# Later requests for feed-forward weight units and a new order of transpositions and copies in a fused GNN, attention and feed-forward kernel

## The reference

```python
def _fff(x, node_w, node_b, w1, b1, w2, b2):
    ...
    for _ in range(DEPTH):                      # 4 levels: a leaf of 16 for every row
        pw = node_w[cur]
        score = jnp.einsum('nd,nd->n', xf, pw) + node_b[cur]
        cur = 2 * cur + 1 + (score >= 0).astype(jnp.int32)
    leaf = cur - N_NODES
    sel = jax.nn.one_hot(leaf, N_LEAVES, dtype=xf.dtype)
    hidden_all = jax.nn.relu(jnp.einsum('nd,ldh->lnh', xf, w1) + b1[:, None, :])
    hidden = hidden_all * sel.T[:, :, None]
    out = jnp.einsum('lnh,lho->no', hidden, w2) + sel @ b2
...
attn = jax.nn.softmax(jnp.einsum('bqd,bkd->bqk', q, k) * scale, axis=-1)
return jnp.einsum('bqk,bkd->bqd', attn, v)
```

## Time and profile before

| | |
|---|---|
| median of 3 runs | 715.13 us (715.1 to 717.05) |
| the profiled execution | 714.04 us |
| its span, first to last instruction | 712.3 us |
| PE (matmul) busy | 694.5 us, 97% |
| DVE (VectorE) busy | 478.6 us, 67% |
| ACT (ScalarE) busy | 403.2 us, 57% |
| POOL (GpSimd) busy | 253.2 us, 36% |
| granted TensorE clock | 1.0 in every stretch |

### The profile page before, as it was taken

The page is one execution under the profiler, slowest core; times in us unless marked ns, Lnnn a source line. Parts: engine busy times, 40 slices in busy tenths (PEclk is TensorE's granted clock), DMA queues, the critical chain, the costliest instruction groups (busy, mean ns, idle before and its releaser), DMA issues.

```text
span 712.3 us, 11790 instructions
## 1 busy us (share of the span) xinstructions
PE 694.5 (97%) x4447; PEld 654.9 (92%) x4447; DVE 478.6 (67%) x965; ACT 403.2 (57%) x702; POOL 253.2 (36%) x232
## 2 busy tenths in 40 slices
PE   8999999999999999999999999999999899989998
PEld 8899999998999999999999999998899897869896
DVE  6778766784777477766666566658675567786744
ACT  5555646555565465758686775522432666675541
POOL 5744312222232322227122263654006841341240
PEclk9999999999999999999999999999999999999999
DMA  6832563422323223231312242333167879997242
GB/s 234 330 115 91 206 237 121 177 90 93 122 104 119 88 92 119 93 119 60 119 59 86 85 183 93 131 122 118 60 237 264 277 297 380 357 363 282 104 155 98
DMA packets 25096, 115.39 MB, mean 162 GB/s; under 512 B 7248, under 2 KB 7680, under 8 KB 15968
## 3 DMA queue, kind: packets, MB, share of 16 engines
q1 hardware_dynamic: 14144, 85.05, 32.5%
q0 software_dynamic: 10464, 29.39, 11.6%
q10 hardware_dynamic: 432, 0.20, 0.1%
HBM read 99.35 MB, written 22.49 MB: 171 GB/s over the span
## 4 chain that ended last, share of the span: by engine, by line
PE 82%; DVE 9%; ACT 4%; DMA 3%; issue 1%; POOL 1%; ACTq 0%; POOLq 0%; DVEq 0%
PE g_bank L1928 35%; PE g_bank L1953 12%; PE o_bank L2005 5%; PE t_bank L1994 4%; DVE w_lo L1265 3%; PE s_bank L2291 2%; PE s_bank L1982 2%; PE s_bank L1983 2%; PE s_bank L2572 2%; PE g_bank L1882 2%; PE t_bank L2291 2%; DMA b_raw<-leaf_b_dram 2%; PE s_bank L2521 1%; PE s_bank L2520 1%; PE s_bank L2519 1%; ACT w_hi L777 1%
## 5 line engine op out<-in xcount | busy, mean ns | idle before, releaser
L1928 PE MATMUL g_bank<-act_hi,w_hi 128*128 128x384 f32 x488 | 169.4, 347 | 0.2 <-DVE v_st L1292 0.2
L1928 PE MATMUL g_bank<-act_hi,w_lo 128*128 128x384 f32 x488 | 163.7, 335 | 0.0
L1928 PE MATMUL g_bank<-act_lo,w_hi 128*128 128x384 f32 x488 | 163.3, 335 | 0.0
L777 ACT ACTIVATE w_hi<-raw 128x2048 fp32r<-128x2048 f32 x67 | 128.2, 1914 | 49.6 <-PE s_bank L2291 12.5
L1265 DVE TENSOR_TENSOR w_lo<-raw,w_hi 128x2048 fp32r<-128x2048 f32 x58 | 135.8, 2341 | 30.1 <-ACT w_hi L777 29.3
L533 POOL DMA_INDIRECT edge_table<-ew,eidx x51 | 66.6, 1306 | 165.2 <-DMA edge_table<-ew,eidx 159.1
L1928 PEld LDWEIGHTS g_bank<-act_hi,w_hi 128*128 128x128 f32 x488 | 91.8, 188 | 3.1 <-issue 3.0
L1928 PEld LDWEIGHTS g_bank<-act_lo,w_hi 128*128 128x128 f32 x488 | 91.9, 188 | 0.0
L1928 PEld LDWEIGHTS g_bank<-act_hi,w_lo 128*128 128x128 f32 x488 | 91.6, 188 | 0.0
L476 POOL TENSOR_TENSOR w_lo<-raw,w_hi 128x2048 fp32r<-128x2048 f32 x10 | 47.6, 4764 | 98.4 <-ACT w_hi L777 94.2
L1404 DVE TENSOR_TENSOR pT_lo<-t_bank,pT_hi 128x384 fp32r<-128x384 f32 x96 | 50.6, 554 | 33.6 <-ACT pT_hi L870 33.1
(11 more groups left out here) (331 smaller groups left out, 1628.2 us busy)
## 6 DMA issues: line engine op xcount, KB each, us to landing
raw<-wstream_dram SPq DMA_DIRECT2D x68, 1024.0 KB, 4.9
xg<-xs POOLq DMA_DIRECT2D x12, 512.0 KB, 7.6
ys<-y_ring POOLq DMA_DIRECT2D x12, 512.0 KB, 7.6
yv<-y_ring POOLq DMA_DIRECT2D x12, 256.0 KB, 2.3
key_b<-edge_keys SPq DMA_DIRECT2D x1, 1728.0 KB, 10.9
x_sb<-x_dram SPq DMA_DIRECT2D x3, 512.0 KB, 5.3
key_a<-edge_keys SPq DMA_DIRECT2D x1, 1536.0 KB, 6.9
y_acc<-x_dram POOLq DMA_DIRECT2D x3, 512.0 KB, 5.3
```

The costliest lines, as they stand in the source:

```text
L777: nc.scalar.activation(flat(w_hi[to][:, :, :]), raws[s], ACT.Copy).then_inc(w_hi_ready, 1)
L1928: last = mm(out, w2[a], x2[b], start=k == 0 and a + b == 0, stop=not after and k == KT - 1 and a == 1)
```

## The change

Four edits. SP gets further waits ahead of feed-forward units: k's second-layer unit u waits for u + 1 finished pairs of k's first layer; v's first-layer units 1, 2 and 3 for 6, 10 and 11 finished second-layer pairs (k's six, then q's); v's second-layer units 0, 1 and 2 for one, two and three finished pairs of v's first layer. The first two row tiles of k are transposed one and two steps sooner, and ScalarE's second copy of selections is put behind the next weight split and the next tile. q's hidden rows are transposed and copied one pair later, in pair 1, and the bias behind pair 1 goes behind pair 2. The gathered tiles are transposed one pair later each, the last of them in v's pair 0.

```diff
--- before.py
+++ after.py
@@ -459,6 +459,13 @@
                     sp.wait_ge(w_lo_pool, lo_turn(n - 2) + 1)
                 else:
                     sp.wait_ge(w_lo_ready, lo_turn(n - 2) + 1)
+                stage, u = divmod(n - U_SORT, GROUPS)
+                if stage == 1:
+                    sp.wait_ge(h_full, u + 1)
+                elif stage == 3 and u:
+                    sp.wait_ge(y_full, 2 * (PAIRS + (0, 4, 5)[u - 1]))
+                elif stage == 4 and u < 3:
+                    sp.wait_ge(h_full, PAIRS + u + 1)
                 sp.dma_start(raws[raw_slot(n)], wstream[n]).then_inc(raw_in[raw_slot(n)], 16)
             for i, (t, half) in enumerate(LAST):
                 cols = slice(half * 512, half * 512 + 512)
@@ -1162,16 +1169,17 @@
             take_tile(1)
             split_hi(Index(U_SORT + 1))
             take_sel(0)
-            take_sel(1)
-            take_hn(0)
-            take_hn(1)
             split_hi(Index(U_SORT + 2))
 
             for f in range(2):
                 i0, n0 = PAIRS * f, U_FIRST[f]
                 for p in range(PAIRS):
+                    if (f, p) == (1, 0):
+                        take_tile(BACK + 2)
                     if 0 < p < PAIRS - 1:
                         take_tile(tile_of_pair(i0 + p + 1))
+                    if (f, p) == (0, 1):
+                        take_sel(1)
                     if p + f == 1:
                         split_hi(Index(n0 + 3))
                     if p in (NT, PAIRS - 1):
@@ -1186,6 +1194,9 @@
                         leaf_bias(4, b2_st)
                     take_h(i0 + p)
                     if (f, p) == (0, 1):
+                        take_hn(0)
+                        take_hn(1)
+                    if (f, p) == (0, 2):
                         leaf_bias(1, b2_st)
                 for b in ((0, 1), (2,))[f]:
                     u0 = U_SECOND[b]
@@ -1213,8 +1224,8 @@
                             take_sel(2 + 2 * b)
                         if b == 1 and p in (0, 2):
                             take_tile(PAIRS + p // 2)
-                        if b == 1 and p >= NT:
-                            take_tile(BACK + p - NT)
+                        if b == 1 and p > NT:
+                            take_tile(BACK + p - NT - 1)
                         if (b, p) == (1, 3):
                             leaf_bias(3, b1_st)
 
@@ -1801,7 +1814,7 @@
                         split_lo(Index(n0 + GROUPS + p // 4))
                     if p:
                         take_hT(2 * i0 + p - 1)
-                    if p == 1:
+                    if (f, p) in ((0, 2), (1, 1)):
                         leaf_bias(1 + 3 * f, b2_st)
                 for b in ((0, 1), (2,))[f]:
                     u0 = U_SECOND[b]
@@ -2417,10 +2430,10 @@
                             leaf_mask(i, t_bank[i][:, 0:N], u=0).then_inc(g_full, 1)
                     if (u, m, k) == (1, 0, 3):
                         count()
-                    if (u, m, k) == (3, 1, 2):
+                    if (u, m, k) == (3, 1, 1):
                         taken(fill_of(Index(U_FFN + 1)))
                         pair_T(0)
-                    if (u, m, k) == (3, 1, 7):
+                    if (u, m, k) == (3, 1, 5):
                         pair_T(1)
 
                 gemm_T(n, act_hi, act_lo, after=leaf_mask, between=in_first, free=fill_of(n).value() if u == 1 else None)
@@ -2531,8 +2544,10 @@
                     def in_pair(k):
                         if k == (6 + f if p else 7) and p < PAIRS - 2:
                             pair_T(tile_of_pair(i0 + p + 2))
-                        if (f, p, k) == (0, 0, 3):
+                        if (f, p, k) == (0, 1, 1):
                             q_hidden_rows()
+                        if (f, p, k) == (1, 0, 2):
+                            pair_T(BACK + 2)
                         if (f, p) == (0, 0) and k in (2, 5):
                             sel_T(k // 4)
                         if (f, p, k) == (1, 0, 4):
@@ -2554,8 +2569,8 @@
                                 hidden_T(PAIRS + p - 1)
                             if b == 1 and half == 1 and p in (0, 2):
                                 pair_T(PAIRS + p // 2)
-                            if b == 1 and half == 1 and p >= NT:
-                                pair_T(BACK + p - NT)
+                            if b == 1 and half == 1 and p > NT:
+                                pair_T(BACK + p - NT - 1)
                             if b == 2 and half == 0:
                                 back_T(p)
```

## The result

| | before | changed |
|---|---|---|
| median, 20 runs each | 714.59 us (713.43 to 717.05) | 717.45 us (713.66 to 721.2) |
| ratio, 95% interval | | 1.0045 [1.0033, 1.0056] |
| the profiled execution | 714.04 us | 717.75 us |
| its span | 712.3 us | 716.0 us |
| mean granted clock of that execution | 1.0 | 0.994 |

The change makes the kernel slower by 0.45%, 3.2 us by the ratio (the two medians differ by 2.9). A faster kernel, 712.4 us, had been forecast, with slower at 8 in 100. The profiled execution is 3.7 us longer than that of before.

A forecast was written before the change was run, and what follows sets the result against it. TensorE bounds the kernel and only its waits can be won: -1.5 (k's first layer), -1.7 (gathered tiles) and +0.5 (SP's gates) make -2.7 us, from a median of 715.13 to 712.4 us; range 710.4 to 715.3.

The forecast's parts named there:

- k's first layer: k's first layer by pairs: -0.1, -1.9, -1.0 and +1.5, sum -1.5 us, bounds 0 and -3.0.
- the young load of the first row tile: Ahead of k's pair 0: first transposition, one step sooner, may wait 0 to 0.52 us for its load; 0.35 taken.
- Rival D: k's first layer: bias wait doesn't return in pair 3; 1.5 us more gained, 710.9 us; chance 0.12.
- q's hidden rows: GpSimd's scatters take 1.0 us each, rows land at 589.2, before TensorE wants them at 590.4; term 0.
- Rival A: q's hidden rows come late, scatters as slow as before: +2.4 us, 714.8 us, no change; chance 0.12.
- The gathered tiles: Around the gathered k tiles: gather wait goes whole, 1.9 us wait ahead of tile 2, next row tile at 638.1; -1.7 us.
- The waits on SP: SP's gates on feed-forward units: v's unit 2 lands in 7.0 us where 6.5 is needed; +0.5 us, ends 0 and +2.7.
- rival B: v's unit 2 lands like the slowest unit before, 9.2 us: 2.2 us beyond the term, 714.6 us; chance 0.14.
- Rival C: v's pair 0: unit 2 later still, slower, deciding from 11.9 us of landing; 718.8 us at 13.4; chance 0.08.

The follow-up runs named there:

- run 5: Kernel before with k's new order alone, gathered tiles in old places, no new SP waits: 712.05 against 714.08 us, ratio 0.9971.
- run 3: The change without SP's waits ahead of v's first-layer units 1 to 3: 715.02 against 714.91 us for the kernel before, ratio 1.0010.
- run 6: The change with gathered tiles in old places and no waits ahead of v's first-layer units: 711.64 us, ratio 0.9972 to the kernel before.
- run 12: The change without v's first-layer waits, k's second bias behind pair 4, store of y tile 8 ahead of the masks: 713.81 us, ratio 1.0009 to before.
- 11: Kernel before with k's new order, k's second bias behind pair 4, store of y tile 8 ahead of the masks: 710.73 us, ratio 0.9961.
- run 1: The change with all its edits of order but without SP's new waits: 716.02 against 714.91 us for the kernel before, ratio 1.0022.
- run 4: The change with the three gathered tiles in their old places: 714.17 against 714.91 us for the kernel before, ratio 0.9991.
- run 13: The change without SP's new waits, v's first bias behind gathered tile 0, next bias request one store later: 717.08 us, ratio 1.0024 to before.
- run 14: Fastest version (ratio 0.9961) with gathered tiles one pair later and v's first bias behind gathered tile 0: 715.48 us, ratio 1.0010 to before.
- run 15: run 14 with the store of y tile 7 issued ahead of the three gathers: 716.25 against 715.41 us for the kernel before, ratio 1.0014.
- run 2: Kernel before with SP's new waits alone, old order: 716.08 against 714.91 us, ratio 1.0013.
- Run 7: The change with 24 unused identity transpositions on TensorE ahead of gathered tile 2: 715.72 us, ratio 1.0035 to the kernel before.
- run 10: The change with GpSimd's store of y tile 8 ahead of the masks: 717.04 against 713.75 us for the kernel before, ratio 1.0053.
- run 16: Fastest version (ratio 0.9961) with the store of y tile 7 ahead of the three gathers: 714.42 us, ratio 0.9994 to the kernel before.
- run 9: run 5 with the bias of k's second layer behind pair 4: 711.60 against 713.75 us for the kernel before, ratio 0.9964.

## Why the prediction was wrong, step by step

**k's first layer: right.** Row tile 3 without a wait, 0.45 us ahead of the second selection (forecast 0.45), 0.36 ahead of tile 4 (0.3), 1.12 ahead of tile 5 (about 1.2). The term of -1.5 measured -2.1 us in run 5. In the profile k's second layer begins 2.2 us sooner. By pairs, from the starts of row tiles 2 to 5 in the two profiles, the forecast -0.1, -1.9, -1.0 and +1.5 came out as -0.6, -2.1, -0.9 and +1.3. The largest miss is the first: 0.35 us had been set down for the young load of the first row tile, and it cost nothing (the first selection is transposed at 558.71, before at 558.96). Two small slips of the working changed nothing: its own numbers give 0.4 us, not 0.45, ahead of the second selection, so the match there is in part luck; and ScalarE's copy of y ends at 624.4, not 624.3. Rival D (the bias is covered) didn't happen.

**q's hidden rows: right.** The three scatters took 0.98, 0.99 and 0.98 us where they had taken 2.29, 3.09 and 1.71, the load started at 579.44 and landed 9.8 us later, at the forecast 589.2, and TensorE never waited for it. Rival A falls. No VectorE instruction with both inputs in SBUF ran beside these three. This again speaks against the inference of the Trainium skill ("SBUF — State Buffer", Who interferes with whom) that such an instruction doesn't hold descriptor generation.

**The gathered tiles: this step failed.** The prediction read: "So tile 2 is transposed at 635.1 with 1.9 us of wait, and the next row tile at [...] 638.1, against 639.79 before: -1.7 us." Measured: +2.7 to +3.9 us by four pairs of runs (3 and 6: 2.7; 12 and 11: 3.4; 1 and 5: 3.6; the change and 4: 3.9). The chain of VectorE behind the bias was counted rightly (10.6 us from y10 to T11, measured 10.75 in runs 3 and 12). What was wrong lies at its start and around it:
- The forecast let the chain start as soon as ScalarE was free, "to 626.3". It left out that the bias passes through GpSimd's two masks, and that these stand behind three gather issues, a store and a load. In the change the masks run from 621.78 to 625.86; one of them took 2.90 us instead of 1.03, with VectorE's split (622.38 to 624.96) beside it. y10 came 9.57 us after T7, in runs 3 and 12 10.45 and 11.35, not 8.4.
- The premise was that the wait for the gather "goes whole". It covered other things that take as long. Pair 4's result needs the ring slot of tile 7, whose store GpSimd asks for right behind the gathers; with the bias moved away, VectorE waited for that store (runs 13 and 14), and with the store moved ahead, for the next (run 15). The waits trade places; in the change GpSimd issues the gathers, two loads or stores, the masks and the next two stores one after another from 616.95 to 626.9, and the stores take 6.4 to 10.5 us to land.
- At the other end the new order needs 2.2 us more from y10 to T11, since one more tile stands between them. In the runs at full clock y10 comes at most 1.7 us sooner behind T7 (run 3). So at its best, runs 3 and 12, the new order breaks even with before, and k's gain is used up on the way.

**The waits on SP: under-sized.** The term was +0.5 with ends 0 and +2.7. All the waits together measured +0.9 us alone (run 2), +1.4 with k's order (run 4 less run 5) and +1.6 with all orders (the change less run 1). v's first-layer units alone measured 1.4 us (run 4 less run 6) and 2.5 in the new order (the change less run 3). With 1.2 to 1.6 us of uncertainty on each, only the last is clear of the forecast 0.5. v's unit 2 was the tight one, as said: asked for at 623.4 (forecast 623.7), it landed 8.8 us later, not 7.0. That is near rival B's 9.2. The estimate of 4.4 us for a unit alone, from the Trainium skill ("DMA: Bandwidth & Descriptors", Anatomy of one DMA), was half of it: this unit did not run alone. (That section's fit is for DMAs that GpSimd issues; this one is issued by SP.) The step's reason for 7.0, that other units were away and the gather was just ending, was wrong: v's units 2 and 3 are now asked for within 3.2 us of each other, at 623.4 and 626.6, beside the stores of y, and the DMA share was 0.98 or more from 620 to 640 us. In the kernel before the same two units took 8.2 and 9.2 us; asked for later, they landed no faster. The store of tile 8, asked for at 625.82, took 8.85 us beside them (4.5 in run 3, 4.0 in run 6): a second cause of the same size, that no rival named. The waits of k's and v's second-layer units cost nothing, as forecast (run 6 against run 5).

**Not in the forecast at all: the clock.** From gathered tile 2 to T11 5.23 us passed instead of 3.12. Rival C had the right sign and stage, and put the point where it decides at 11.9 us of landing; with the start 1.2 us late and the clock, 8.8 us was enough.

The account of T7 to T11 in the profiled execution: forecast 19.5 us, start of the chain +1.2, unit and store +1.8 (2.3 less the 0.5 forecast), clock +2.1, the chain itself +0.15, together 24.8; measured 24.8. Before T7, 1.8 of the 2.2 us that k's order had won were gone (618.72 against 619.11): the store of tile 0 took 11.6 us and its successor's copy waited 6.27 us. Other runs with the same waits and k's order had T7 from 616.5 (run 12) to 623.1 (run 4, whose store of tile 0 took 13.3 us), so part of that is one execution's chance; the ratio takes in all 20 executions.

**What stays open.** How much of the ratio the clock is. Run 7's profile shows 2.1 us, its interval can't tell 1.0035 from 1.0045, and the filling matmuls had to end in time themselves. The clocks of all executions give an upper end, an estimate (a stretch at half clock costs at most half of its length, as much as it takes off the mean clock): the mean is 0.9959 over the 20 of the change and 0.9978 over the 134 of the kernel before that ran beside the experiments, and the difference, taken over 716 us, is 1.4 us. So in the mean the clock is less than half of the 3.2 us; the profiled execution, at 0.994, lost more to it than most. The store's and the unit's shares weren't parted: run 3 takes both away at once, and moving the store (run 10) didn't make it land in time.

## What to carry to other kernels

A wait on the engine that bounds the kernel covers other late things; before it is taken away, list for each engine what it would do in that time and what that needs, down to the ring slots, the stores that free them and the queue of the engine that issues them. If three or four of those take as long as the wait, moving the work only names the next one. And a request held back to free bandwidth for others should still stand more than the slowest landing of that stretch ahead of its use: here v's unit 2 stood 6.5 us ahead, and landings took up to 9.2 us before.

## What the hardware showed

- **The clock falls in waits of TensorE that had been harmless when shorter.** Waits of 4.18 us (the change), 3.38 (run 2), 3.59 (run 10), 4.12 (run 13), 3.13 (run 14), 6.86 (run 15) and 3.27 (run 16) were each followed by matmuls at the lower level; those of 1.77 (run 3), 1.93 and 2.56 were not. Near 2 us it goes either way: 2.57 us in run 5 left it at 1.00, 2.01 in run 9 was followed by a window at 0.50, as were, 8 us apart, 2.44 and 1.92 in run 1 (0.50 and 0.57). The wait of 4.18 us in the change cost 6.3: itself and 2.1 us of slow matmuls. All 20 executions of the change had a mean clock below 1.0, but so had 92 of the 134 of the kernel before: its profile, at 1.0 throughout, is one of the better ones.
- **GpSimd's masks** (16 by 1024) took 1.03 us alone. One that started while VectorE's low split ran ended 0.9 us behind the split, in every run's profile of this stretch, and so took 1.7 to 3.2 us; in run 4 both started clear of a split and both took 1.03. The scatters show the same, 0.98 us alone and up to 3.09. The Trainium skill's section named above agrees for the masks, which read SBUF.
- **Landing.** v's units 2 and 3 of 1 MB, asked for late, took 8.8 and 10.1 us (8.2 and 9.2 before); the shortest unit in the kernel before took 4.8. A store of one y tile took from 2.9 to 13.3 us, both in run 4. Requests that are held back aren't gone: the DMA share fell to 0.30 where they had been and stayed at 1.0 where they came to.
